# A cross-attention and FFN kernel: scores and skip product in fp16 halves, x fully normalised, keys scaled per batch

## The chip, the cores and the metric

The kernel runs on one core of a Trainium2 chip, as one launch over 32 batches. The metric is the device time of that launch in microseconds (us), median of several runs; lower is better.

## The reference, cut to what matters

```python
def _L0_xattn_ref(pcd_up, pcd_down, Wq, Wk, Wv, Wskip):     # (32,128,1024), (32,128,256)
    q = einsum('oc,bcn->bon', Wq, pcd_up)
    k = einsum('oc,bcm->bom', Wk, pcd_down)
    v = einsum('oc,bcm->bom', Wv, pcd_down)
    energy = einsum('bcn,bcm->bnm', q, k) / sqrt(128)
    attention = softmax(energy, axis=-1)
    x = einsum('bnm,bcm->bcn', attention, v)
    return einsum('oc,bcn->bon', Wskip, pcd_up) + x

x = x + _L0_xattn_ref(_layernorm(x), ctx_1024, Wq, Wk, Wv, Wskip)
x = x + _L0_ffn_ref(_layernorm(x), qweight, scales, zeros, bias)   # 4 bit weights, 1024 -> 1024
```

All of it is in float32.

## The kernel before, in words

A batch is a 128 x 1024 tile of x and a 128 x 256 tile of context. Wq and Wk are multiplied once into one matrix (`proj[:, KEY]`), so that the scores of a batch are x times (KEY x ctx): 1024 rows by 256 columns, made in eight tiles of 128 x 256, two tiles to a chunk `j` of 0 to 3. The chunks alternate between two PSUM tiles `ps_e`.

Precision is kept by splitting operands into a high and a low part, and adding three products (hi hi, hi lo, lo hi; `HI_LO`). Before the change x minus its mean (`xc`), the keys `k` and the skip weights `wsk` are split into two float32r parts; the inverse standard deviation `rstd1` of the layer norm is folded into the keys (`keys_hi`, `keys_lo`) and into `sk_scale`, and `xc` is only centred. The values `v`, the probabilities and the second normalised x (`xn`) are already split into fp16 parts.

The five engines work on different batches at once. The order of work is written out by hand for each engine (its `run_in` for the first batches, then `step(t)` for t from 2), and semaphores tie them together. In `step(t)` TensorE does, with b = t, n = t + 1, a = t - 1, q = t - 2: `scores(b, 0)`, `keys_values(n)`, `skip_attend(a, 0)`, `scores(b, 1)`, `scores(b, 2)`, `skip_attend(a, 1)`, `scores(b, 3)`, `ffn(q, 0)`, `ffn(q, 1)`. `scores(b, 2)` and `scores(b, 3)` use the PSUM tiles of chunks 0 and 1 again and wait for `exp_done` of these.

A chunk's way is: TensorE `scores` (L889), VectorE `row_max` (L659), ScalarE `exps` (L480, one activation a tile with the row sum), VectorE `invert` (L664), GpSimd `normalise` (L255), ScalarE `probs_hi` (L489), VectorE `probs_lo` (L668), two transposing DMAs of SyncE, and TensorE `skip_attend` of the next step (L915 skip, L919 attention).

The first layer norm's way is: VectorE `stats1`, `aggregate1` (L604), `variance1` (L610), GpSimd `inverse_std1` (L263), and ScalarE `centre` (L435) and `centred_hi` (L442), GpSimd `centred_lo` (L270, for the first batch VectorE's `first_centred_lo`, L639). `centre` needs only the mean, not `inverse_std1`.

VectorE's `value_scale` (L621 to L629, four instructions on 128 x 1) reads the context's maximum summed over partitions, which a one-column matmul (L898) leaves in `ps_m`, but waits for `kv_done`, the end of `keys_values`. The second layer norm goes VectorE `residual` (L678), `stats2`, `aggregate2`, GpSimd `inverse_std2` (L279, L281), ScalarE `apply_norm2` (L498) and `xn_high` (L507), GpSimd `xn_low` (L302), SyncE's transposes and TensorE `ffn` (L924, L928).

Of the kernel before, what the change touches and what calls it, by code (L numbers as in the profile page):

```python
# [15 lines left out]
def xattn_ffn_program(nc, x, ctx_in, wq, wk, wv, wskip, qweight, scales, zeros, bias, out):  # L16
# [26 lines left out]
    with es:  # L43
# [73 lines left out]
        st1_done, mv1_done, ve1_done, rstd1_done = (sem(n) for n in ("st1", "mv1", "ve1", "rstd1"))  # L117
        xc_done, xchi_done, xclo_done = (sem(n) for n in ("xc", "xchi", "xclo"))
# [920 lines left out]
```

## Time and profile before

| | |
|---|---|
| median of 3 runs | 526.82 us (526.39 to 528.74) |
| the profiled execution's own time | 526.57 us |
| its span, first to last instruction | 524.6 us (1.97 us lie around it) |
| mean granted TensorE clock | 0.99 |
| busy: TensorE / GpSimd / VectorE / ScalarE | 95% / 90% / 82% / 71% |

Times in the rows below are counted from the start of the span. TensorE's matmuls are pipelined: one of 512 columns is shown as 0.38 us long while the next starts 0.216 us after it. So what a matmul costs is read from the distance of starts, not from its duration, and a matmul that follows without a wait on another group may be shown a little early.

### The profile page before, as it was taken

What the parts mean: (1) busy time and instruction counts of PE and PEld (TensorE: products, weight loads), DVE (VectorE), ACT (ScalarE), POOL (GpSimd) and SP (SyncE); (2) the same over time, 40 slices, a digit from 0 to 9 for tenths busy, and PEclk for the clock granted to TensorE, in tenths of its full rate; (3) what the DMA queues carried; (4) which work ended last, traced back from release to release, by engine and by line L of the source; (5) the groups of instructions that cost most, each with busy time, mean ns of one, the idle gap of its engine ahead of it and who ended that gap; (6) DMA issues with size and microseconds to landing.
All of it is one profiled execution on the core that took longest, in us unless ns stands there. A gap on an engine that the chain in (4) does not pass through costs nothing.

```text
span 524.6 us, 9213 instructions
## 1 busy us (share of the span) xinstructions
PE 496.9 (95%) x2668; PEld 302.8 (58%) x2668; DVE 427.5 (82%) x981; ACT 372.7 (71%) x844; POOL 470.8 (90%) x717
## 2 busy tenths in 40 slices
PE   4658999999999999999999999999999999999977
PEld 3535565656665565666656566666556666656533
DVE  5899788889888888988888898888888988887632
ACT  4878877777877777777777777777777787776610
POOL 4899899999999999999999999999999999999752
PEclk9889999999999999999999999999999999999999
DMA  8626877797898789779878877887787679655673
GB/s 300 191 69 137 161 196 185 190 194 179 178 184 194 167 187 193 192 171 185 204 163 186 182 195 174 192 202 160 184 182 201 174 179 209 159 134 138 147 142 102
DMA packets 227059, 92.65 MB, mean 177 GB/s; under 512 B 209472, under 2 KB 214080, under 8 KB 227008
## 3 DMA queue, kind: packets, MB, share of 16 engines
q1 hardware_dynamic: 226288, 91.91, 74.5%
q8 instruction: 21, 0.34, 0.3%
q14 instruction: 30, 0.25, 0.1%
q10 hardware_dynamic: 720, 0.14, 0.1%
HBM read 23.87 MB, written 16.78 MB: 77 GB/s over the span
## 4 chain that ended last, share of the span: by engine, by line
PE 86%; POOL 7%; DVE 2%; DMA 2%; issue 1%; ACT 1%; POOLq 0%; SPq 0%
PE ps_y L924 41%; PE ps_e L889 15%; PE ps_o L919 14%; PE ps_o L915 8%; PE ps_kv L900 3%; PE ps_y L928 3%; PE ps_kv L902 2%; POOL sb_prob L255 2%; POOL sb_xc_lo L270 1%; DMA sb_xnt_lo<-sb_xn_lo 1%; DMA sb_x<-in_x_dram 1%; POOL sb_xn_lo L302 1%; ACT sb_prob L480 1%; DVE sb_st L596 0%; ACT sb_wf L512 0%
## 5 line engine op out<-in xcount | busy, mean ns | idle before, releaser
L924 PE MATMUL ps_y<-sb_wf,sb_xnt_hi 128*128 128x512 f16 x512 | 192.1, 380 | 4.4 <-DMA sb_xnt_lo<-sb_xn_lo 3.4
L924 PE MATMUL ps_y<-sb_wf,sb_xnt_lo 128*128 128x512 f16 x512 | 192.0, 379 | 0.0
L480 ACT ACTIVATE sb_prob<-ps_e,sb_neg_max 128x256 f32<-128x256 f32 x256 | 118.3, 470 | 57.2 <-DVE sb_neg_max L659 57.2
L255 POOL TENSOR_SCALAR sb_prob<-sb_prob,sb_rsum 128x256 f32<-128x256 f32 x256 | 122.7, 492 | 15.2 <-DVE sb_rsum L664 15.0
L668 DVE TENSOR_TENSOR sb_p_lo<-sb_prob,sb_p_hi 128x1024 f16<-128x1024 f32 x64 | 78.3, 1223 | 48.8 <-ACT sb_p_hi L489 48.8
L889 PE MATMUL ps_e<-sb_k_hi,sb_xc_hi 128*128 128x256 f32 x256 | 90.8, 355 | 10.4 <-DVE sb_k_lo L647 5.7
L249 POOL TENSOR_TENSOR sb_o<-sb_prod,sb_x 128x512 f32<-128x512 f32 x63 | 80.6, 1279 | 7.0 <-DVE sb_prod L702 7.0
L924 PEld LDWEIGHTS ps_y<-sb_wf,sb_xnt_hi 128*128 128x128 f16 x512 | 49.9, 98 | 63.8 <-DMA sb_xnt_lo<-sb_xn_lo 4.3
L659 DVE TENSOR_REDUCE sb_neg_max<-ps_e 128x2 f32<-128x512 f32 x128 | 84.8, 681 | 1.6 <-PE ps_e L889 1.2
L924 PEld LDWEIGHTS ps_y<-sb_wf,sb_xnt_lo 128*128 128x128 f16 x512 | 50.0, 98 | 56.7
L489 ACT ACTIVATE sb_p_hi<-sb_prob 128x1024 f16<-128x1024 f32 x64 | 67.4, 1053 | 19.8 <-issue 15.5
L270 POOL TENSOR_TENSOR sb_xc_lo<-sb_xc,sb_xc_hi 128x512 fp32r<-128x512 f32 x62 | 79.9, 1289 | 0.0
L498 ACT ACTIVATE sb_xn<-sb_x,sb_nb,sb_rstd 128x1024 f32<-128x1024 f32 x32 | 43.0, 1344 | 51.7 <-POOL sb_nb L281 51.7
L889 PE MATMUL ps_e<-sb_k_lo,sb_xc_hi 128*128 128x256 f32 x256 | 73.5, 287 | 0.0
L889 PE MATMUL ps_e<-sb_k_hi,sb_xc_lo 128*128 128x256 f32 x256 | 73.3, 286 | 0.0
L302 POOL TENSOR_TENSOR sb_xn_lo<-sb_xn,sb_xn_hi 128x512 f16<-128x512 f32 x63 | 71.9, 1162 | 0.1
L889 PEld LDWEIGHTS ps_e<-sb_k_hi,sb_xc_hi 128*128 128x128 f32 x256 | 49.8, 195 | 22.3 <-DVE sb_k_lo L647 11.4
L702 DVE TENSOR_TENSOR sb_prod<-ps_y,sb_scale_row 128x512 f32<-128x512 f32 x64 | 43.8, 684 | 14.6 <-PE ps_y L928 13.9
L889 PEld LDWEIGHTS ps_e<-sb_k_lo,sb_xc_hi 128*128 128x128 f32 x256 | 50.0, 195 | 2.3
L480 ACT ACTIVATION_READ_ACCUMULATOR sb_prob<-ps_e,sb_neg_max 128x1 f32 x256 | 51.1, 200 | 0.0
L678 DVE SCALAR_TENSOR_TENSOR sb_x<-ps_o,sb_o_scale,sb_x 128x512 f32<-128x512 f32 x64 | 47.2, 738 | 3.8 <-PE ps_o L919 3.8
L919 PE MATMUL ps_o<-sb_pt_hi,sb_v_hi 128*128 128x512 f16 x128 | 49.3, 385 | 0.7 <-DMA sb_pt_lo<-sb_p_lo 0.7
(123 smaller groups left out, 926.1 us busy)
## 6 DMA issues: line engine op xcount, KB each, us to landing
sb_x<-in_x_dram SPq DMA_DIRECT2D x32, 512.0 KB, 4.0
out_dram<-sb_o SPq DMA_DIRECT2D x64, 256.0 KB, 2.4
sb_ctx<-in_ctx_dram SPq DMA_DIRECT2D x32, 128.0 KB, 2.7
sb_q<-in_L_ffn_qweight_dram SPq DMA_DIRECT2D x4, 512.0 KB, 9.0
sb_pt_hi<-sb_p_hi SPq DMA_TRANSPOSE x64, 3.0
sb_pt_lo<-sb_p_lo SPq DMA_TRANSPOSE x64, 2.8
sb_scale_row<-in_L_ffn_scales_dram SPq DMA_DIRECT2D x1, 512.0 KB, 10.9
sb_xnt_hi<-sb_xn_hi SPq DMA_TRANSPOSE x32, 2.8
```

Source lines behind the costliest of these rows:

```text
L249: pool.tensor_tensor(o_sb[:, c % 2, cols], prod[:, h, :], x1[:, c % 3, cols], ALU.add).then_inc(out_done[h], 1)
L255: last = pool.tensor_scalar(prob[:, j, t, :], prob[:, j, t, :], rsum[:, j, t:t + 1], P_SCALE, ALU.mult, ALU.mult)
L270: last = pool.tensor_tensor(xc_lo[:, n % 3, cols], xc[:, cols], xc_hi[:, n % 3, cols].bitcast(F32), ALU.subtract)
L302: last = pool.tensor_tensor(xn_lo[:, k:k + KT // 2, :], xn[:, k:k + KT // 2, :], xn_hi[:, k:k + KT // 2, :], ALU.subtract)
L480: done = act.activation(prob[:, j, t, :], ps_e[j % 2][:, t, :], ACT.Exp, bias=neg_max[:, j, t:t + 1], accum_out=esum[:, j, t:t + 1])
L489: act.activation(p_hi[:, h, :, :].rearrange("n k (t m) -> n k t m", m=P), prob[:, 2 * h:2 * h + 2, :, :].rearrange("n j t (k m) -> n k (j ...
L659: dve.tensor_reduce(neg_max[:, j, :], ps_e[j % 2][:, :, :], AX.X, ALU.max, negate=True).then_inc(max_done[j], 1)
L668: dve.tensor_tensor(p_lo[:, h, :, :].rearrange("n k (t m) -> n k t m", m=P), prob[:, 2 * h:2 * h + 2, :, :].rearrange("n j t (k m) -> n k ...
L678: dve.scalar_tensor_tensor(x1[:, a % 3, cols], ps_o[h][:, :], o_scale[:, a % 3:a % 3 + 1], x_sb[:, a % 4, cols], ALU.mult, ALU.add).then_i ...
L889: last = pe.matmul(ps_e[j % 2][:, t, :], xc_p[s][:, b % 3, cols], k_p[m][:, b % 2, :], start=i == 0, stop=i == 2)
L919: last = pe.matmul(ps_o[h][:, :], v_p[s][:, a % 3, k * P:(k + 1) * P], pt_p[m][:, h, k, :], start=False, stop=k == MT - 1 and i == 2)
L924: pe.matmul(ps_y[h][:, :], xnt_p[s][:, q % 2, kt, :], wf[:, kt, h * HALF:(h + 1) * HALF], start=kt == 0 and s == 0, stop=False)
```

## The change

x is now normalised fully, times 1024: `centre` has `rstd1` as scale and the product mean x rstd x -1 (`nb1`, from the new `negated_mean1` on VectorE) as bias. Keys and skip weights no longer carry `rstd1`. They get a per-batch scale from a bound on their size, which a second one-column matmul makes; the four instructions of `value_scale` become three of `range_scales`. `xc`, `k` and `wsk` are split into fp16 halves in place of float32r. As the scores come out scaled, `exps` multiplies by `top` (a scale operand of 128 x 1) and first makes the scaled negated maximum `neg_top` by one small activation for each chunk, for which it waits itself. Scaling of the two weights moves to GpSimd. The order of the run-in changes on ScalarE, VectorE and GpSimd.

```diff
-        xc_hi, xc_lo = (sb(n, [P, 3, N], F32R) for n in ("xc_hi", "xc_lo"))
-        k_hi, k_lo = (sb(n, [P, 2, M], F32R) for n in ("k_hi", "k_lo"))
+        xc_hi, xc_lo = (sb(n, [P, 3, N], F16) for n in ("xc_hi", "xc_lo"))
+        k_hi, k_lo = (sb(n, [P, 2, M], F16) for n in ("k_hi", "k_lo"))
-        wsk_hi, wsk_lo = (sb(n, [C, 3, C], F32R) for n in ("wsk_hi", "wsk_lo"))
+        wsk_hi, wsk_lo = (sb(n, [C, 3, C], F16) for n in ("wsk_hi", "wsk_lo"))
...
+            def scale_weights():                                   # GpSimd, was on VectorE
+                pool.wait_ge(w_step, 5)
+                for w in (wv_sb, wskip_sb):
+                    pool.tensor_scalar(w[:, :], w[:, :], rw[:, :], None, ALU.mult).then_inc(w_scaled, 1)
...
                 inverse_std1(0)
+                scale_weights()
                 zero_point_quotient()
...
                 normalise(0, 3)
+                inverse_std1(2)
                 zero_point_remainder()
-                inverse_std1(2)
...
             def centre(n):
-                act.wait_ge(mv1_done, n + 1)
+                act.wait_ge(nb1_done, n + 1)
                 if ran(n, 1):
                     act.wait_ge(xclo_done, n)
-                act.activation(xc[:, :], x_sb[:, n % 4, :], ACT.Identity, bias=mv1[:, 0:1],
-                               scale=-1.0).then_inc(xc_done, 1)
+                act.activation(xc[:, :], x_sb[:, n % 4, :], ACT.Identity, bias=nb1[:, :],
+                               scale=rstd1[:, :]).then_inc(xc_done, 1)
...
             def exps(b, j):
                 act.wait_ge(max_done[j], b + 1)
                 if ran(b, 1):
                     act.wait_ge(plo_done[j // 2], b)
+                top = t_scale[:, b % 3, 1:2]
+                act.activation(neg_top[:, j, :], neg_max[:, j, :], ACT.Copy, scale=top).then_inc(top_done, 1)
+                act.wait_ge(top_done, CHUNKS * b + j + 1)
                 for t in range(TPC):
-                    done = act.activation(prob[:, j, t, :], ps_e[j % 2][:, t, :], ACT.Exp,
-                                          bias=neg_max[:, j, t:t + 1], accum_out=esum[:, j, t:t + 1])
+                    done = act.activation(prob[:, j, t, :], ps_e[j % 2][:, t, :], ACT.Exp, scale=top,
+                                          bias=neg_top[:, j, t:t + 1], accum_out=esum[:, j, t:t + 1])
...
             def run_in():                                          # ScalarE
-                centre(0)
+                first_centre(0)
                 first_centred_hi(0)
                 keys_hi(0)
+                first_centre(1)
                 first_centred_hi(1)
                 keep_projections()
-                centre(1)
                 exps(0, 0)
                 exps(0, 1)
+                centre(1)
                 centred_hi(1)
...
+            def negated_mean1(m):                                  # VectorE
+                dve.wait_ge(rstd1_done, m + 1)
+                if ran(m, 1):
+                    dve.wait_ge(xc_done, m)
+                dve.tensor_scalar(nb1[:, :], mv1[:, 0:1], rstd1[:, :], -1.0, ALU.mult,
+                                  ALU.mult).then_inc(nb1_done, 1)
...
-            def value_scale(n):
-                dve.wait_ge(kv_done, n + 1)
+            def range_scales(n):
+                dve.wait_ge(bound_done, n + 1)
+                if n == 0:
+                    dve.wait_ge(floors_made, 2)
+                    dve.wait_ge(w_step, 5)
+                t = t_scale[:, n % 3, :]
+                dve.tensor_tensor(t, (ps_o[0] if n == 0 else ps_m)[:, HALF - 2:HALF], floors[:, :],
+                                  ALU.max).then_inc(t_step, 1)
+                dve.wait_ge(t_step, 3 * n + 1)
+                dve.reciprocal(t_inv[:, n % 2, :], t).then_inc(t_step, 1)
+                dve.tensor_scalar(o_scale[:, n % 3:n % 3 + 1], t_scale[:, n % 3, 0:1], w_inv[:, :], None,
                                   ALU.mult).then_inc(t_step, 1)
-                dve.wait_ge(t_step, 4 * n + 3)
-                dve.wait_ge(rstd1_done, n + 1)
-                dve.tensor_scalar(sk_scale[:, :], v_scale[:, :], rstd1[:, n % 2:n % 2 + 1], P_SCALE, ALU.mult,
...
+            def key_bound():
+                dve.wait_ge(key_kept, 1)
+                dve.tensor_reduce(kmax[:, :], proj[:, KEY, :], AX.X, ALU.max,
+                                  apply_absolute_value=True).then_inc(kmax_done, 1)
+                dve.wait_ge(kmax_done, 1)
+                dve.tensor_scalar(kmax_row[:, :], kmax[:, 0:1].broadcast_to((P, P)), 1.0 / V_TOP, None,
+                                  ALU.mult).then_inc(kmax_done, 1)
...
                 keep_key()
+                key_bound()
+                negated_mean1(0)
                 context_max(0)
-                scale_weights()
+                weight_norms()
+                range_scales(0)
                 first_centred_lo(0)
...
                 row_max(1, 0)
+                negated_mean1(2)
...
                     invert(b, 1)
+                if ran(m):
+                    negated_mean1(m)
                 if ran(n):
                     keys_lo(n)
...
+            def bound(n, to):                                      # TensorE
+                pe.wait_ge(amax_done, n + 1)
+                peak = amax[:, n % 2:n % 2 + 1]
+                pe.matmul(to[:, HALF - 2:HALF - 1], top_inv[:, :], peak, start=True, stop=True)
+                pe.matmul(to[:, HALF - 1:HALF], kmax_row[:, :], peak, start=True, stop=True).then_inc(bound_done, 1)
```

`keys_hi(n)` now waits for `t_step` (the reciprocal in `range_scales`) where it waited for `rstd1_done`; `weight_norms` is the old reductions without the scaling, with one more reduction. For batch 0 `first_centre` and `first_centred_hi` work on halves of 512 columns. From batch 2 on `keys_values(n)` calls `bound(n, ps_m)` where it had its one-column matmul; for batch 1 `second_keys` does.

## Rows read from the trace of the kernel before

**Rows 1.** The page's first part: busy time, share, instructions.
```profile
PE 496.9 (95%) x2668; PEld 302.8 (58%) x2668; DVE 427.5 (82%) x981; ACT 372.7 (71%) x844; POOL 470.8 (90%) x717
```

**Rows 2.** Windows view, 60 to 490 us: busy by engine, PEclk, DMA.
```profile
60.00:490.00 430.00, 430.00 (x2346) 262.26 (x2346) 365.22 (x842) 319.61 (x738) 405.26 (x592) 1.00 0.79 182
```

**Rows 3.** The chain that ended last, in order of time, three places.
```profile
53.34 1.04 PE ps_y L924 x4
...
203.05 3.47 PE ps_y L924 x16
...
218.26 3.47 PE ps_y L924 x16
```

**Rows 4.** Waits in total, times, longest, window 60 to 490 us.
```profile
ACT sb_prob L480 <- DVE sb_neg_max L659: 55.8, 85, 1.8
...
DVE sb_t_scale L621 <- PE ps_kv L902: 8.1, 26, 0.3
```

**Rows 5.** Timeline of TensorE within one batch: start, duration.
```profile
202.89 0.39 PE L924 MATMUL ps_y<-sb_wf,sb_xnt_hi 128*128 128x512 f16 x1
203.12 0.38 PE L924 MATMUL ps_y<-sb_wf,sb_xnt_lo 128*128 128x512 f16 x1
...
206.57 0.38 PE L924 MATMUL ps_y<-sb_wf,sb_xnt_hi 128*128 128x512 f16 x1
...
209.81 0.38 PE L924 MATMUL ps_y<-sb_wf,sb_xnt_lo 128*128 128x512 f16 x1
...
210.95 0.18 PE L898 MATMUL ps_m<-sb_amax,sb_ones 128*128 128x1 bf16 x1
210.99 0.68 PE L900 MATMUL ps_kv<-sb_ctx,sb_proj 128*128 128x256 f32 x2
...
213.74 0.38 PE L919 MATMUL ps_o<-sb_pt_hi,sb_v_lo 128*128 128x512 f16 x1
...
214.07 0.28 PE L889 MATMUL ps_e<-sb_k_lo,sb_xc_hi 128*128 128x256 f32 x1
...
215.26 0.28 PE L889 MATMUL ps_e<-sb_k_hi,sb_xc_lo 128*128 128x256 f32 x1
215.38 0.40 PE L915 MATMUL ps_o<-sb_xc_hi,sb_wsk_hi 128*128 128x512 f32 x1
...
216.09 0.39 PE L919 MATMUL ps_o<-sb_pt_hi,sb_v_hi 128*128 128x512 f16 x1
```

**Rows 6.** Groups of instructions, 60 to 490 us, ScalarE and GpSimd: busy, mean ns, idle before.
```profile
L480 ACT ACTIVATE sb_prob<-ps_e,sb_neg_max 128x256 f32<-128x256 f32 x230 | 106.3, 471 | 55.8 <-DVE sb_neg_max L659 55.8
L489 ACT ACTIVATE sb_p_hi<-sb_prob 128x1024 f16<-128x1024 f32 x56 | 58.9, 1052 | 13.6 <-issue 13.6
...
L498 ACT ACTIVATE sb_xn<-sb_x,sb_nb,sb_rstd 128x1024 f32<-128x1024 f32 x28 | 37.6, 1344 | 41.6 <-POOL sb_nb L281 41.6
L435 ACT ACTIVATE sb_xc<-sb_x,sb_mv 128x1024 f32<-128x1024 f32 x27 | 30.8, 1141 | 0.0
...
L255 POOL TENSOR_SCALAR sb_prob<-sb_prob,sb_rsum 128x256 f32<-128x256 f32 x226 | 105.9, 481 | 12.1 <-DVE sb_rsum L664 11.9
...
L270 POOL TENSOR_TENSOR sb_xc_lo<-sb_xc,sb_xc_hi 128x512 fp32r<-128x512 f32 x56 | 71.3, 1273 | 0.0
L302 POOL TENSOR_TENSOR sb_xn_lo<-sb_xn,sb_xn_hi 128x512 f16<-128x512 f32 x58 | 66.2, 1162 | 0.0
```

**Rows 7.** Timelines around chunk 1's exponentials and VectorE's `residual`.
```profile
201.41 0.20 ACT L480 ACTIVATION_READ_ACCUMULATOR sb_prob<-ps_e,sb_neg_max 128x1 f32 x1
...
202.30 0.28 PE L889 MATMUL ps_e<-sb_k_lo,sb_xc_hi 128*128 128x256 f32 x1
...
214.42 0.75 DVE L678 SCALAR_TENSOR_TENSOR sb_x<-ps_o,sb_o_scale,sb_x 128x512 f32<-128x512 f32 x1
```

**Rows 8.** Timelines of ScalarE and GpSimd in the run-in.
```profile
14.75 1.06 ACT L442 ACTIVATE sb_xc_hi<-sb_xc 128x1024 fp32r<-128x1024 f32 x1
...
14.26 1.84 POOL L255 TENSOR_SCALAR sb_prob<-sb_prob,sb_rsum 128x256 f32<-128x256 f32 x4 [1.06 <-DVE sb_rsum L664]
```

More of the change, by code:

```diff
@@ L58, in xattn_ffn_program @@
         proj = sb("proj", [C, 3, C])
-        wsum, wmax, rw, w_inv = (sb(n, [C, 1]) for n in ("wsum", "wmax", "rw", "w_inv"))
+        wsum, wskip_max, wmax, rw, w_inv, kmax = (sb(n, [C, 1]) for n in ("wsum", "wskip_max", "wmax", "rw", "w_inv", "kmax"))
         ident, ident16 = sb("ident", [P, P]), sb("ident16", [P, P], BF16)
-        ones = sb("ones", [P, P], BF16)
+        top_inv, kmax_row = sb("top_inv", [P, P], BF16), sb("kmax_row", [P, P], BF16)
+        floors = sb("floors", [P, 2])
         neg_half = sb("neg_half", [P, 1])
@@ L116, in xattn_ffn_program @@
         src_done, rows_turned, rows_done, seed_made = sem("src"), sem("rows_turned"), sem("rows"), sem("seed_made")
[L117 to L118 removed]
+        st1_done, mv1_done, ve1_done, rstd1_done, nb1_done = (sem(n) for n in ("st1", "mv1", "ve1", "rstd1", "nb1"))
+        xc0_done, xc_done, xchi_done, xclo_done = (sem(n) for n in ("xc0", "xc", "xchi", "xclo"))
+        kmax_done, bound_done, top_done = sem("kmax"), sem("bound"), sem("top")
         amax_done, kv_done, t_step, kvhi_done, kvlo_done = (sem(n) for n in ("amax", "kv", "t_step", "kvhi", "kvlo"))
@@ L470, in values_hi @@
                     act.wait_ge(attn_done[1], n - 2)
-                act.activation(wsk_hi[:, n % 3, :], proj[:, SKIP, :], ACT.Copy, scale=sk_scale[:, :])
+                act.activation(wsk_hi[:, n % 3, :], proj[:, SKIP, :], ACT.Copy, scale=t_inv[:, n % 2, 0:1])
                 act.activation(v_hi[:, n % 3, :], ps_kv[:, M:2 * M], ACT.Copy,
-                               scale=v_scale[:, :]).then_inc(kvhi_done, 1)
+                               scale=t_inv[:, n % 2, 0:1]).then_inc(kvhi_done, 1)
             def exps(b, j):
@@ L754, in run_in @@
                 invert(0, 0)
-                value_scale(0)
+                range_scales(1)
+                negated_mean1(1)
                 invert(0, 1)
@@ L786, in run_in @@
                 variance1(3)
-                value_scale(2)
+                range_scales(2)
                 residual(0, 1)
@@ L792, in run_in @@
                 aggregate2(0)
+                negated_mean1(3)
                 keys_lo(2)
@@ L807, in step @@
                 if ran(n):
-                    value_scale(n)
+                    range_scales(n)
                 if t == 2:
@@ L868, in _ @@
             pe.wait_ge(ident_made, 2)
+            pe.wait_ge(kmax_done, 2)
+            bound(0, ps_o[0])
             pe.wait_ge(w_scaled, 2)
@@ L894, in keys_values @@
                 pe.wait_ge(ctx_loaded[n % 2], nth(n, 2))
-                pe.wait_ge(amax_done, n + 1)
                 if ran(n, 1):
                     pe.wait_ge(kvlo_done, n)
-                pe.matmul(ps_m[:, HALF - 1:HALF], ones[:, :], amax[:, n % 2:n % 2 + 1], start=True, stop=True)
                 if n > 1:
+                    bound(n, ps_m)
                     pe.matmul(ps_kv[:, 0:M], proj[:, KEY, :], ctx_sb[:, n % 2, :], start=True, stop=True)
@@ L908, in second_keys @@
                 pe.matmul(ps_y[0][:, 0:M], proj[:, KEY, :], ctx_sb[:, 1, :], start=True, stop=True).then_inc(k1_done, 1)
+                bound(1, ps_m)
             def skip_attend(a, h):
```

91 lines of the change are left out of this document (42 added, 49 removed).

## The prediction

> **What bounds the kernel now.** I read the page's busy shares first [rows 1]: TensorE 95%, GpSimd 90%. Then the windows view of the middle [rows 2]: in those 430 us TensorE is busy all the time at full granted clock, GpSimd 405.26 us (94%), VectorE 85%, ScalarE 74%. Busy matmuls overlap, so this alone doesn't say that TensorE is the bound; the waits do: in this window no wait of TensorE for another engine is listed, while ScalarE waits 55.8 us for row maxima [rows 4] and 41.6 us for the second norm [rows 6]. And the chain that ended last runs through TensorE and repeats exactly: the first half of an `ffn` starts at 203.05 and again at 218.26 [rows 3], so a batch takes 15.21 us, and 430 us hold 28.3 batches. The reader should see two things: time taken out of TensorE's stream comes out of the total, once for each batch; and the others have little room, GpSimd above all.
>
> The first `ffn`, that of step 2, is on the chain from 53.34 [rows 3]. Before it TensorE waits for a run-in in which GpSimd is the bound; after it come the steps 3 to 31, 29 of them with scores.
>
> **What the change takes out of TensorE's stream.** Distances of starts [rows 5]:
> - fp16, 512 columns: 206.57 to 209.81 is 15 steps, 0.216 us each.
> - float32r, 256 columns: 214.07 to 215.26 is 10 steps, 0.119 us each.
> - float32r, 512 columns: 215.38 to 216.09 is 3 steps, 0.237 us each; I take 0.235.
>
> The trace has no fp16 matmul of 256 columns. From below it is half of 0.216, 0.108 us; from above it is what float32r takes, 0.119 (if the weight load or something fixed sets it). The 512 wide ones show a dearer float32r column at equal width (0.235 against 0.216), which a fixed cost for each matmul wouldn't halve at 256 but does (0.019 and 0.011), so I take 0.108. 24 score matmuls a batch x 0.011 = 0.26 us. Six skip matmuls x 0.019 = 0.11 us. Where the stream goes from float32 types to fp16, the first fp16 step is 0.23 (202.89 to 203.12) in place of 0.216; three times a batch, 0.01 each: 0.03 us.
>
> Weighed against this: the Trainium skill (TensorE: Matmul & The Clock Gate, Back-to-back issue gap) says that a warm matmul costs its columns at 2.4 GHz plus 2.5 ns. By it a 256 wide fp16 step is 0.109 us, and the saving of the scores 0.24 in place of 0.26; the trace's 0.216 for 512 columns agrees with it.
>
> Added: the second one-column matmul. The first costs 0.04 us (210.95 to 210.99 [rows 5]). The second has other weights to load behind so short a matmul, so it costs between 0.04 and one small matmul's whole duration, 0.18. I take 0.08. Net: 0.26 + 0.11 + 0.03 - 0.08 = 0.32 us a batch, bounds -0.04 (scores no faster, second column matmul 0.18) and 0.36 (that matmul 0.04). Period 14.89. Over 29 steps: 9.3 us.
>
> **What the others get, and what hides it.**
> GpSimd: 405.26 us in 28.3 batches is 14.33 a batch. `centred_lo` gets the operand types that `xn_low` has, so 1162 in place of 1273 ns [rows 6], twice a batch: 0.22 less. In the steady part `scale_weights` doesn't run and `inverse_std1` is as before. Its idle time without the waits for `invert` [rows 6], (430 - 405.26 - 11.9) / 28.3 = 0.45 a batch, are small gaps between chained one-column instructions and stay. So it needs 14.56, under 14.89. Bound: no saving, 14.78.
>
> VectorE: `sk_scale` goes, `negated_mean1` comes, both about 0.2 us. `range_scales` waits for the one-column matmuls, not for `keys_values`: a wait of 0.3 us (8.1 us in 26 [rows 4]) goes, and with the instruction that goes VectorE reaches `residual(a, 0)` about 0.5 earlier. `negated_mean1(m)` stands behind `invert(b, 1)`, when `inverse_std1(m)` has long been done; `keys_lo` and `values_lo` stand behind it and have slack of microseconds. Free, as VectorE has 15% idle.
>
> ScalarE: the small activation before each chunk. Not in the trace. Below: 0.20, the read of the accumulator [rows 7]; above: 0.47, a 256 column exponential [rows 6]. From 1052 ns at 1024 columns without a 128 x 1 operand and 471 - 89 at 256 (next sentence) a column costs 0.87 ns and the rest 0.16, plus 0.09 for the operand: 0.25. With its own wait I take 0.30. Each exponential has a second 128 x 1 operand: `centre` with one takes 1141 ns, `probs_hi` without 1052 ns, both 1024 columns, so 0.09 each; bounds 0 and 0.20 (the 1344 of `apply_norm2`, with two and a row sum, less 1141). Sum for ScalarE: 4 x 0.30 + 9 x 0.09 = 2.0 us a batch. Its waits are (55.8 + 41.6 + 13.6) / 28.3 = 3.9 us a batch [rows 4, 6], less the 0.32 that the batch shrinks: it fits with 1.6 us to spare. A wait for the maximum is now followed by 0.30 + 2 x 0.09 = 0.48 more before `exp_done`.
>
> The Trainium skill (ScalarE: Activation LUTs, What ACT_TABLE_LOAD costs) speaks against this part of the change in the same way: each pointer operand adds some 93 ns. By it ScalarE's extra comes to about 2.0 us too, and the 89 ns between the rows agrees.
>
> Who waits for `exp_done`? TensorE, before `scores(b, 3)` for chunk 1. Now the last read of the accumulator ends at 201.41 + 0.20 = 201.61, and `scores(b, 3)` starts at 202.30 less one step, 202.18 [rows 7]: slack 0.57 us. Measured from `scores(b, 0)`, the need comes 18 x 0.011 + 0.11 + 0.02 - 0.08 = 0.25 sooner. The maximum can come sooner as well: it stands behind `residual(a, 0)`, which starts at 214.42 though its matmul ended at 213.74 + 0.38 = 214.12 [rows 5, 7]; VectorE's 0.5 lets it start there: 0.3. So slack 0.57 - 0.48 - 0.25 + 0.3 = 0.14 us. No stall, but barely. For chunk 0 there is more: `keys_values`, half of the skip and attention and `scores(b, 1)` lie between.
>
> **The run-in.** Its end is set by GpSimd, which from 14.26 us on [rows 8] has hardly a gap until about 50 us. Changes: `keys_hi(0)` now needs `key_bound` (two instructions of about 0.3), the weight norms (one reduction more) and `range_scales(0)` on VectorE, and `centre` needs `inverse_std1` and `negated_mean1`. Step by step with the durations of the same instructions: the first scores come about 0.85 later; the second half of `first_centred_lo`, and with it `stats1(1)` and the first row maximum, about 1.5 later; the first exponential 1.4 later, and GpSimd's first `normalise` at 15.5 in place of 14.26. `centre(1)` then stands behind two chunks of exponentials: `centred_hi(1)` starts near 17.7 in place of 14.75, `centred_lo(1, 0)` some 2.7 later. Chunks 2 and 3 stand behind that on ScalarE, and GpSimd waits for them; `centre(2)` stands behind `negated_mean1(2)`, itself behind the maximum of batch 1. I get `normalise(1, 0)` 3.6 to 4 us late. GpSimd gets back six times 0.11 by 50 us. I take +3.5 us; bounds +0.8 (only the first scores' delay) and +5.
>
> **Sum.** 526.57 (this execution; the median is 0.25 more) - 9.3 + 3.5 = 520.8. This is the likeliest, with 516.5 to 524.5 as its own range (0.25 to 0.37 a batch, gain 7.3 to 10.7; run-in 0.8 to 5).
>
> **Rivals.**
> A. *The exponentials' chain becomes the bound* (slower). Place: `scores(b, 3)` waits for `exp_done` of chunk 1. For: slack of 0.14 only. Against: ScalarE and VectorE each have slack elsewhere. At the upper bounds (small activation 0.47 and 0.05 for its wait, operands 0.20 each) 0.92 is added in place of 0.48, which is 0.30 more than the slack of 0.14 takes: a stall of 0.30 a batch, 8.8 us, 529.6. It makes the kernel slower than before from a stall of 0.20, 0.82 added. Chance 0.14.
> B. *GpSimd becomes the bound.* If `centred_lo` is no faster (14.78) and its waits for `invert`, 11.9 us or 0.42 a batch [rows 6], stay in part, its period is 14.95 to 15.20: gain 7.5 to 0.3, time 522.6 to 529.8, middle 526. For: 94% busy. Against: the same types run at 1162 ns. Chance 0.12.
> C. *A 256 column matmul is no cheaper in fp16*, so that the change doesn't do in the scores what it says: 0.06 a batch, 1.8 us, time 528.3. Chance 0.06.
> D. *The run-in hardly costs*: the first maxima come late, but ScalarE has its first exponentials earlier in its order than `centre(1)`, and if GpSimd's small zero-point steps fill its waits, only +0.8 stays: 518. Chance 0.14.
> Chance of the likeliest 0.54.
>
> **How the numbers follow.** A measurement of this kernel tells a change of about 0.5%, 2.6 us. Faster by more than that means under 524.2: the likeliest (0.50 of 0.54), D (0.14), the near end of B (0.04): 0.68. Within: the rest of the likeliest (0.04), most of B (0.06), most of C (0.04), the small stalls of A (0.02): 0.16. Slower than 529.2: A with its stall near the bound (0.12), and the far ends of B and C (0.04): 0.16. Range for 8 in 10: from 515, as the run-in and the steps could both come out at their best, to 528, which leaves out A at its bound and the far ends.
>
> **What the profile after would show.** Right: starts of score matmuls 0.108 to 0.109 apart, skip 0.216; period 14.85 to 14.9; no wait of TensorE in the window 60 to 490; `centred_lo` near 1160 ns; exponentials near 560 ns and four small activations near 0.28; the first `ffn` 3 to 4 us later than 53.34. Wrong: a regular gap of TensorE ahead of `scores(b, 3)` released by ScalarE (A), period over 14.95 with GpSimd without a gap (B), 0.119 steps (C), a first `ffn` by 54.5 (D).

## The result, and the profile after

The changed kernel takes 546.33 us, median of 4 runs (546.22 to 546.45), beside 527.57 us (526.39 to 528.74) for the kernel before: ratio 1.036, 95% interval 1.033 to 1.038. It is slower by 19 us, where 520.8 was predicted. The profiled execution took 546.41 us, its span is 544.5. Two executions of run 13 below (587 and 588 us, granted clock 0.84 in place of 0.98) and one of run 11 (2917 us) were in a slower state, and are not counted.

First part of the page after, then the windows view of 60 to 490 us, against [rows 1, 2]:

```profile
PE 491.4 (90%) x2668; PEld 265.9 (49%) x2700; DVE 420.8 (77%) x982; ACT 433.8 (80%) x973; POOL 481.0 (88%) x721
...
ACT 34%; DVE 20%; issue 17%; POOL 15%; PE 2%; DMA 1%; SPq 0%; ACTq 0%; another core or an unknown queue 0%; POOLq 0%
```

```profile
60.00:490.00 430.00, 413.06 (x2276) 224.55 (x2302) 348.78 (x819) 361.77 (x817) 402.08 (x576) 1.00 0.83 176
```

TensorE now has gaps, and makes up 2% of the chain that ended last, which [rows 3] showed running through its `ffn`. No engine is busy all the time: ScalarE has the largest share of the chain, 34%, and is busy 361.77 of 430 us. So I looked for a loop over several engines: each waits for the one before it, and none is busy throughout.

The period is read from the distance of one instruction of each batch, GpSimd's bias of the second norm (`inverse_std2`, L281 before, L289 after). Its timeline after:

```profile
106.29 1.26 POOL L289 TENSOR_SCALAR sb_nb<-sb_mv,sb_rstd 128x1 f32<-128x1 f32 x1
...
483.34 1.26 POOL L289 TENSOR_SCALAR sb_nb<-sb_mv,sb_rstd 128x1 f32<-128x1 f32 x1
```

24 batches lie between: 15.71 us each, where the kernel before has 15.22 (99.51 to 479.91 us, 25 batches). And the view of this tile, with shortest, median and longest duration in ns and the first and last start, has the first at 42.4 us where before it was at 38.1 (second line):

```profile
L289 POOL TENSOR_SCALAR sb_nb<-sb_mv,sb_rstd x32: 267/1258/1264, 42.4 to 527.1; 128x1 f32<-128x1 f32 x32
```

```profile
L281 POOL TENSOR_SCALAR sb_nb<-sb_mv,sb_rstd x32: 265/748/752, 38.1 to 506.2; 128x1 f32<-128x1 f32 x32
```

So the run-in costs 4.3 us and the 31 periods behind it 16.6 (484.7 less 468.1); the tail gives 1 back. (The prediction named another sign of the run-in, the part of the first `ffn` that starts at 53.34 [rows 3]: it starts at 57.79 after, 4.5 later.)

The groups that answer to [rows 6], 60 to 490 us, and the waits of the same window:

```profile
L492 ACT ACTIVATE sb_prob<-ps_e,sb_neg_top,sb_t_scale 128x256 f32<-128x256 f32 x217 | 120.6, 560 | 3.6
...
L278 POOL TENSOR_TENSOR sb_xc_lo<-sb_xc,sb_xc_hi 128x512 f16<-128x512 f32 x54 | 62.5, 1157 | 0.0
...
L289 POOL TENSOR_SCALAR sb_nb<-sb_mv,sb_rstd 128x1 f32<-128x1 f32 x27 | 34.0, 1259 | 2.7
L489 ACT ACTIVATE sb_neg_top<-sb_neg_max,sb_t_scale 128x2 f32<-128x2 f32 x109 | 32.1, 294 | 23.1 <-DVE sb_neg_max L687 23.0
```

```profile
PEld ps_e L932 <- ACT sb_prob L492: 30.1, 47, 1.4
DVE sb_rsum L692 <- ACT sb_prob L492: 28.9, 54, 0.6
ACT sb_neg_top L489 <- DVE sb_neg_max L687: 23.0, 54, 0.6
PE ps_e L932 <- ACT sb_prob L492: 13.5, 24, 0.9
```

The single costs came out near what was worked out: an exponential 560 ns (predicted 471 + 89), the small activation 294 (predicted 0.28 to 0.30), `centred_lo` 1157 (1162). TensorE's wait for the exponentials is there, as rival A had it. The row to look at is the second wait: VectorE's `invert` waits for the exponentials 54 times in 27 batches, twice in each. And `nb` of the second norm takes 1259 ns where it took 748, though nothing in it changed.

Timelines of VectorE, ScalarE and GpSimd after, around the last chunk of a batch. In brackets stands the idle time before an instruction and what ended it:

```profile
197.39 0.17 DVE L692 RECIPROCAL sb_rsum<-sb_esum 128x2 f32<-128x2 f32 x1
197.47 0.73 DVE L706 SCALAR_TENSOR_TENSOR sb_x<-ps_o,sb_o_scale,sb_x 128x512 f32<-128x512 f32 x1
198.12 0.68 DVE L687 TENSOR_REDUCE sb_neg_max<-ps_e 128x2 f32<-128x512 f32 x1
...
200.40 0.17 DVE L692 RECIPROCAL sb_rsum<-sb_esum 128x2 f32<-128x2 f32 x1 [0.56 <-ACT sb_prob L492]
200.48 1.21 DVE L696 TENSOR_TENSOR sb_p_lo<-sb_prob,sb_p_hi 128x1024 f16<-128x1024 f32 x1
```

```profile
198.83 0.30 ACT L489 ACTIVATE sb_neg_top<-sb_neg_max,sb_t_scale 128x2 f32<-128x2 f32 x1 [0.43 <-DVE sb_neg_max L687]
...
200.17 0.20 ACT L492 ACTIVATION_READ_ACCUMULATOR sb_prob<-ps_e,sb_neg_top,sb_t_scale 128x1 f32 x1
201.85 1.36 ACT L510 ACTIVATE sb_xn<-sb_x,sb_nb,sb_rstd 128x1024 f32<-128x1024 f32 x1 [1.49 <-POOL sb_nb L289]
```

```profile
199.91 0.55 POOL L287 TENSOR_TENSOR sb_rstd<-sb_ve,sb_neg_half 128x1 f32<-128x1 f32 x1 [0.21 <-DVE sb_ve L721]
200.56 1.26 POOL L289 TENSOR_SCALAR sb_nb<-sb_mv,sb_rstd 128x1 f32<-128x1 f32 x1
```

The same place before, VectorE, ScalarE and GpSimd:

```profile
203.57 0.67 DVE L659 TENSOR_REDUCE sb_neg_max<-ps_e 128x2 f32<-128x512 f32 x1
...
205.12 0.15 DVE L693 TENSOR_SCALAR sb_ve<-sb_mv 128x1 f32<-128x1 f32 x1
205.33 0.17 DVE L664 RECIPROCAL sb_rsum<-sb_esum 128x2 f32<-128x2 f32 x1
205.41 1.21 DVE L668 TENSOR_TENSOR sb_p_lo<-sb_prob,sb_p_hi 128x1024 f16<-128x1024 f32 x1
```

```profile
205.09 0.20 ACT L480 ACTIVATION_READ_ACCUMULATOR sb_prob<-ps_e,sb_neg_max 128x1 f32 x1
```

```profile
206.00 0.75 POOL L281 TENSOR_SCALAR sb_nb<-sb_mv,sb_rstd 128x1 f32<-128x1 f32 x1
```

From the start of `row_max(b, 3)` to that of `invert(b, 3)` it is 1.76 us before and 2.28 after: 0.52 more, the small activation with its hand-over (0.33) and two operands (0.18). Before, VectorE came to this `invert` just as the exponentials ended (205.27 and 205.29), with no idle time and no slack either. After, it idles 0.56 us there, and all that stands behind it in its order moves: `probs_lo(b, 0)`, `context_max`, `scale_product(q, 0)`. GpSimd's `nb`, which starts beside `probs_lo`, ends 0.13 us after it (201.82 and 201.69), as before (206.75 and 206.62). So it too follows the exponentials, and `apply_norm2`, which ScalarE has in its order ahead of the next batch's work, starts at 201.85.

The whole loop stands in the chain of waits of after, in order of time (start, us), here with its middle:

```profile
301.00 0.30 ACT sb_neg_top L489
...
303.55 0.95 ACT sb_xc_hi L457
304.50 0.19 ACT sb_neg_top L489
...
305.18 0.75 ACT sb_prob L492 x3
...
307.37 0.17 DVE sb_rsum L692
307.53 0.65 DVE sb_x L706
...
309.89 0.56 POOL sb_rstd L287
...
310.54 1.27 POOL sb_nb L289
...
311.83 0.91 ACT sb_xn L510
...
313.27 0.96 ACT sb_p_hi L501
...
315.39 0.68 DVE sb_prod L730
```

Chunk 0's exponentials, ScalarE's high parts, chunks 1 and 2, `invert`, `residual(a, 1)`, the second norm, `apply_norm2`, `probs_hi`, `probs_lo`, `scale_product`, and the row maximum of the next chunk 0. TensorE is not in it. Chunk 3's exponentials are not in it either, as this view follows semaphores: by the rows above they come in through `probs_lo`, with whose end `nb` ends.

### The profile page after: what moved, and what is told of

It reads as the page before. It is cut to its first block, busy times and chain, and to the rows that moved or that the text cites. A ratio compares the mean times of both kernels' runs of the same rounds, so it can differ in the third digit from the quotient of the medians.

```text
span 544.5 us, 9380 instructions
## 1 busy us (share of the span) xinstructions
PE 491.4 (90%) x2668; PEld 265.9 (49%) x2700; DVE 420.8 (77%) x982; ACT 433.8 (80%) x973; POOL 481.0 (88%) x721
## 4 chain that ended last, share of the span: by engine, by line
ACT 34%; DVE 20%; issue 17%; POOL 15%; PE 2%; DMA 1%; SPq 0%; ACTq 0%; another core or an unknown queue 0%; POOLq 0%
ACT sb_prob L492 11%; POOL sb_nb L289 7%; ACT sb_xn L510 6%; ACT sb_p_hi L501 5%; ACT sb_xc_hi L457 5%; DVE sb_neg_max L687 4%; DVE sb_x L706 4%; DVE sb_st L711 4%; DVE sb_prod L730 4%; POOL sb_prob L259 4%; POOL sb_rstd L287 3%; ACT sb_neg_top L489 3%; PE ps_y L967 2%; DVE sb_rsum L692 2%; ACT sb_k_hi L472 2%
## 5 line engine op out<-in xcount | busy, mean ns | idle before, releaser
L492 ACT ACTIVATE sb_prob<-ps_e,sb_neg_top,sb_t_scale 128x256 f32<-128x256 f32 x256 | 142.3, 560 | 4.2
L259 POOL TENSOR_SCALAR sb_prob<-sb_prob,sb_rsum 128x256 f32<-128x256 f32 x256 | 124.9, 501 | 21.2 <-DVE sb_rsum L692 18.2
L932 PE MATMUL ps_e<-sb_k_hi,sb_xc_hi 128*128 128x256 f16 x256 | 71.8, 280 | 29.5 <-ACT sb_prob L492 17.8
L278 POOL TENSOR_TENSOR sb_xc_lo<-sb_xc,sb_xc_hi 128x512 f16<-128x512 f32 x62 | 72.7, 1173 | 1.2 <-ACT sb_xc_hi L457 1.1
L932 PE MATMUL ps_e<-sb_k_lo,sb_xc_hi 128*128 128x256 f16 x256 | 71.3, 278 | 0.0
L932 PE MATMUL ps_e<-sb_k_hi,sb_xc_lo 128*128 128x256 f16 x256 | 71.3, 278 | 0.0
L489 ACT ACTIVATE sb_neg_top<-sb_neg_max,sb_t_scale 128x2 f32<-128x2 f32 x128 | 37.6, 294 | 29.8 <-DVE sb_neg_max L687 29.7
L692 DVE RECIPROCAL sb_rsum<-sb_esum 128x2 f32<-128x2 f32 x128 | 19.7, 154 | 45.2 <-ACT sb_prob L492 42.9
L932 PEld LDWEIGHTS ps_e<-sb_k_hi,sb_xc_hi 128*128 128x128 f16 x256 | 25.4, 99 | 58.7 <-ACT sb_prob L492 36.0
## 6 DMA issues: line engine op xcount, KB each, us to landing
sb_scale_row<-in_L_ffn_scales_dram SPq DMA_DIRECT2D x1, 512.0 KB, 10.5
```

Source lines behind the costliest of these rows:

```text
L259: last = pool.tensor_scalar(prob[:, j, t, :], prob[:, j, t, :], rsum[:, j, t:t + 1], P_SCALE, ALU.mult, ALU.mult)
L492: done = act.activation(prob[:, j, t, :], ps_e[j % 2][:, t, :], ACT.Exp, scale=top, bias=neg_top[:, j, t:t + 1], accum_out=esum[:, j, t:t ...
L932: last = pe.matmul(ps_e[j % 2][:, t, :], xc_p[s][:, b % 3, cols], k_p[m][:, b % 2, :], start=i == 0, stop=i == 2)
```

## The experiments

Two theories. **L**: the loop over VectorE, ScalarE and GpSimd has taken TensorE's place; what counts is where a step stands. **S**: the rival; what counts is ScalarE's work in sum, wherever it stands. The first four runs ask before that whether it is the exponentials at all.

**1. The exponentials as before.** `exps` of after without the small activation and without the scale operand. Here and in runs 2, 3, 5 and 6 the softmax is left unscaled, so the output differs. That this doesn't set the time is seen from runs 4 and 8, which show the same two things with the right softmax.

```diff
-                top = t_scale[:, b % 3, 1:2]
-                act.activation(neg_top[:, j, :], neg_max[:, j, :], ACT.Copy, scale=top).then_inc(top_done, 1)
-                act.wait_ge(top_done, CHUNKS * b + j + 1)
...
-                    done = act.activation(prob[:, j, t, :], ps_e[j % 2][:, t, :], ACT.Exp, scale=top,
-                                          bias=neg_top[:, j, t:t + 1], accum_out=esum[:, j, t:t + 1])
+                    done = act.activation(prob[:, j, t, :], ps_e[j % 2][:, t, :], ACT.Exp,
+                                          bias=neg_max[:, j, t:t + 1], accum_out=esum[:, j, t:t + 1])
```

> The changed kernel with the exponentials of the kernel before: no small activation, no scale operand (the scores stay unscaled inside the softmax, so its output differs). Theory L: a loop over VectorE and ScalarE (row maximum, exponentials of chunks 1 and 3, then the reciprocal that stands in VectorE's order ahead of the values' low half and of the probabilities' low half, the second norm, ScalarE's second norm application, the next batch) sets the period of 15.71 us; each of chunks 1 and 3 gives back 0.33 + 2 x 0.09 = 0.51, so the loop needs 14.69 and TensorE's own 14.87 is the bound: about 519 to 522 us. Rival G: GpSimd or the transposes set the period (nb2 takes 1.26 us, transposes land in 4.2 us): over 538 us. Rival R: the run-in alone has the loss: it stays over 540.

517.58 us, ratio to the kernel before 0.983 (0.979 to 0.987); period 14.88. The whole loss and more, 28.8 us, is in these lines (L had 519 to 522). Its windows view and the chain in shares:

```profile
60.00:490.00 430.00, 428.10 (x2398) 241.66 (x2426) 365.14 (x853) 329.26 (x750) 406.54 (x607) 1.00 0.86 185
```

```profile
PE 81%; POOL 5%; DVE 4%; ACT 3%; issue 3%; DMA 2%; SPq 1%; another core or an unknown queue 0%; POOLq 0%; ACTq 0%; DVEq 0%
```

TensorE is the bound again, and what the prediction says of its stream holds: 14.88 against 14.89 predicted.

**2 and 3. One of the two at a time.** Run 2 keeps the scale operand alone (a column of ones), run 3 the small activation alone, with its wait.

```diff
+                    ... ACT.Exp, scale=one_col[:, :], bias=neg_max[:, j, t:t + 1], ...          # run 2
...
+                act.activation(neg_top[:, j, :], neg_max[:, j, :], ACT.Copy, scale=one_col[:, :]).then_inc(top_done, 1)
+                act.wait_ge(top_done, CHUNKS * b + j + 1)                                         # run 3
```

> The changed kernel without the small activation and its wait, but with a scale operand of 128 x 1 (a column of ones; output differs). Theory L: the loop gets back 2 x 0.33, period 15.05, 31 periods: 526 us. Rival W (only the wait on itself stalls ScalarE, the operand is free): 521. Rival G: over 538.

> The changed kernel with the small activation and its wait, and the exponentials with an immediate scale (the small one multiplies by a column of ones; output differs). Theory L: the loop gets back 4 x 0.09, period 15.35: 535 us. Rival W: 546, nothing is got back. Rival G: over 538.

Run 2: 524.0 us, 0.994 (0.992 to 0.996), period 15.01, 2 us under what was expected. Run 3: 529.0, 1.004 (1.002 to 1.006), period 15.16, 6 us under it. Over run 1 the two cost 6.4 and 11.4 us, 17.8 in sum, and 28.8 together. So each alone seems first to use up slack that the two must share; runs 5 and 6 say how much.

**4. The same on the kernel before.** Both steps added there, with a scale of one: float32r, keys and `value_scale` as they were.

> The kernel before, with the small activation (times a column of ones) and the scale operand (ones) added, same results. Theory L: its loop is at most 0.3 us under its period of 15.21 (VectorE's wait for the end of keys and values), so 1.02 added gives 15.9 to 16.2: 545 to 556 us. The prediction's view (0.57 us of slack at TensorE, ScalarE with 3.9 us idle): 527 to 530. Rival G or R: 527.

550.8 us, 1.045 (1.041 to 1.049), period 15.88. This is the prediction's own step, tried alone. It held the step to be covered, which would give 527 to 530; it costs 24 us.

**5 and 6. Which chunks.** Both steps (with ones) on chunks 1 and 3 alone, and on chunks 0 and 2 alone; the others as in run 1. Each has half of ScalarE's extra work.

```diff
+                if j in (1, 3):          # run 6: (0, 2)
+                    act.activation(neg_top[:, j, :], neg_max[:, j, :], ACT.Copy, scale=one_col[:, :]).then_inc(top_done, 1)
...
+                else:                    # the exponentials as before
```

> The changed kernel with small activation and scale operand (times a column of ones) on chunks 1 and 3 alone; chunks 0 and 2 have the exponentials of the kernel before (output differs). Theory L (only the chunks whose reciprocal VectorE waits for ahead of the values' low half and of the probabilities' low half count): period near 15.6 to 15.7, 543 to 546 us. Rival S (ScalarE's whole work of a batch counts, all chunks alike): halfway between 517.6 and 546.3, 532 us.

> The same on chunks 0 and 2 alone (output differs). Theory L: period 14.9 to 15.0, 518 to 521 us. Rival S: 532 us.

On 1 and 3: 535.49 us, 1.015 (1.013 to 1.018), period 15.47. On 0 and 2: 520.37, 0.986 (0.984 to 0.989), period 14.87, TensorE's own. The same work costs 2.8 us over run 1 at one place and 17.9 at the other, so S falls. L's numbers hold for 0 and 2, but chunks 1 and 3 were to cost nearly all (543 to 546), and cost 17.9 of 28.8. The timeline of run 5 tells why the other two chunks count once these are there (ScalarE, then VectorE):

```profile
313.72 0.29 ACT L493 ACTIVATE sb_neg_top<-sb_neg_max,sb_one_col 128x2 f32<-128x2 f32 x1 [0.29 <-DVE sb_neg_max L695]
```

```profile
300.73 0.48 DVE L690 SCALAR_TENSOR_TENSOR sb_v_lo<-ps_kv,sb_t_inv,sb_v_hi 128x256 f16<-128x256 f32 x1
301.13 0.15 DVE L700 RECIPROCAL sb_rsum<-sb_esum 128x2 f32<-128x2 f32 x1
```

Chunk 1's step waits 0.29 us for VectorE: chunk 0's 0.52 more on ScalarE would cost 0.23 here. And `invert(b, 2)` doesn't wait for chunk 2, it follows `values_lo` without idle time: part of chunk 2's 0.52 is covered there too. Chunks 1 and 3 show no such cover. If they have none, the loop without any extra is 15.47 - 2 x 0.52 = 14.43 us, by run 5. This is an estimate: no run shows the loop at that length, as TensorE sets the period then. The others by it: run 1, 14.43, under TensorE's 14.88, so TensorE sets it (measured 14.88); run 6, with the 0.24 that after has over run 5, 14.7, under it as well (14.87); run 3, with 0.33 in place of 0.52, 14.43 + 0.66 and a few hundredths for chunks 0 and 2, 15.1 to 15.2 (15.16); run 2, with 0.18, 14.8, so TensorE's 14.88 (15.01, more than both). Most of what is missing there stands in VectorE's `wsk_lo`, which lies ahead of `invert(b, 2)` in its order: in the mean it takes 517 ns in run 2, 420 in run 3, 345 in run 5 and 344 after, though it is the same instruction in all of them. With its 0.17, run 2 comes to 14.96. With all four it is 15.71, 0.24 over run 5, where 0.23 for chunk 0 and something more for chunk 2 was to be expected. By the same reckoning the kernel before had a loop of some 15.88 - 1.04 - 0.24 = 14.6 us (run 4), 0.6 under its 15.22: single waits without slack don't yet make a loop without slack.

**7, 9 and 10. Other orders of VectorE's steps.** If `invert` holds up what stands behind it, another order should bring the loss back. All three are the changed kernel otherwise. Run 7: `negated_mean1`, `keys_lo` and `values_lo` ahead of `invert(b, 1)`, and `probs_lo(b, 0)` ahead of `invert(b, 3)`. Run 9: `context_max` and `scale_product(q, 0)` between `invert(b, 3)` and `probs_lo(b, 0)`. Run 10: run 9, and `invert(b, 1)` behind `values_lo`, `invert(b, 2)` behind `residual(a, 1)` and `row_max(b, 3)`.

> The changed kernel, all of it, but in VectorE's step the reciprocal of chunk 1 comes after keys_lo and values_lo, and that of chunk 3 after probs_lo(b, 0); keys_lo waits for kvhi_done so that the two engines don't read one bank at once. Same results. Theory L: both in-order waits (0.50 and 0.56 us a batch) leave the loop, period 14.9 to 15.1, 521 to 527 us. Rival S: 546, the work on ScalarE is the same. Rival G (normalise comes later, GpSimd takes over): 530 to 540.

542.83 us, 1.029 (1.027 to 1.032), period 15.61: only 3.5 us of it. L's 521 to 527 is far off, and the time alone lies between G's 530 to 540 and S's 546, of which runs 5 and 6 exclude S. `probs_lo` now lies on the other small step of GpSimd (VectorE, then GpSimd):

```profile
214.00 1.22 DVE L696 TENSOR_TENSOR sb_p_lo<-sb_prob,sb_p_hi 128x1024 f16<-128x1024 f32 x1
```

```profile
214.16 1.46 POOL L287 TENSOR_TENSOR sb_rstd<-sb_ve,sb_neg_half 128x1 f32<-128x1 f32 x1
...
215.72 0.27 POOL L289 TENSOR_SCALAR sb_nb<-sb_mv,sb_rstd 128x1 f32<-128x1 f32 x1
```

The power, 0.55 us elsewhere, takes 1.46, and `nb` 0.27. So what was saved in one was lost in the other, as far as these rows go.

> The changed kernel, all of it, but in VectorE's step context_max and scale_product(q, 0) come between the reciprocal of chunk 3 and probs_lo(b, 0). Same results. Theory L2 (the loop runs through chunks 0, 1 and 2 on ScalarE, residual, second norm; and its last link, GpSimd's nb2 of 0.27 us, is stretched to 1.26 because it starts while VectorE's probs_lo runs and ends with it): nb2 is back to about 0.27, the loop loses 1.0, period 14.9 to 15.1, 521 to 527 us. Rival H (nb2 is not held by probs_lo but slow for another reason, or ScalarE's work sets the period): nb2 stays over 0.7 and the time over 540.

535.84 us, 1.015 (1.012 to 1.018), period 15.35. With `probs_lo` out of the way of both steps the second norm comes about 1 us sooner, and 10.5 us come back: this link was real, and H is out. But the time is 9 us over L2's range, not at TensorE's bound. GpSimd's groups in the window:

```profile
L253 POOL TENSOR_TENSOR sb_o<-sb_prod,sb_x 128x512 f32<-128x512 f32 x56 | 97.8, 1747 | 2.3 <-DVE sb_prod L730 2.2
...
L299 POOL CAST sb_xn_lo<-sb_rs 128x3 bf16<-128x3 f32 x28 | 33.0, 1180 | 0.0
L289 POOL TENSOR_SCALAR sb_nb<-sb_mv,sb_rstd 128x1 f32<-128x1 f32 x28 | 7.4, 264 | 2.8
```

`nb` is down from 1259 to 264 ns, but `write_out`'s product now lies beside `probs_lo` and went from 1272 to 1747 twice a batch, and a three-column cast takes 1180, which took 0.20 (L299 at 203.91 us after). GpSimd is busy 410.9 of 430 us and has 41% of the chain that ended last (15% after), so it is most of the next bound; VectorE's `invert` still waits 31.6 us for exponentials.

> The same, and the reciprocals of chunks 1 and 2 stand behind values_lo and behind residual(a, 1) and row_max(b, 3), so that no exponential lies ahead of the second norm in VectorE's order (keys_lo waits for kvhi_done). Same results. Theory L2: TensorE's bound, period 14.87 to 14.95, 520 to 523 us. Rival G (normalise of chunks 1 and 2 comes later and GpSimd sets the period): 15.1 or more, over 526.

550.0 us, 1.043 (1.040 to 1.046), period 15.86: in rival G's range, not L2's. GpSimd's `normalise` needs these `invert`s, and now waits for them 30.9 us in the window (11.4 after), while GpSimd is busy 391.69 of 430 us only. So not its own work sets the period but its waits, which this order adds: something waits for these `invert`s on each side.

**8, 11, 12 and 13. The halves without scaled exponentials.** Run 8 has the fp16 halves, but x times 4 in place of 1024 and the keys times 1/4, with no per-batch bound: the scores come out in their own size and `exps` is that of before. The second one-column matmul, `key_bound` and the key scale go.

```diff
+    X1_SCALE = 4.0
-                dve.tensor_scalar(ve1[:, :], mv1[:, 1:2], EPS, XN_SCALE ** -2 ...
+                dve.tensor_scalar(ve1[:, :], mv1[:, 1:2], EPS, X1_SCALE ** -2 ...
...
-                dve.tensor_scalar(proj[:, KEY, :], ps_o[0][:, 0:C], SM_SCALE / XN_SCALE, None,
+                dve.tensor_scalar(proj[:, KEY, :], ps_o[0][:, 0:C], SM_SCALE / X1_SCALE, None,
```

> fp16 halves without scaled exponentials: x normalised times 4, keys divided by 4 and unscaled, so the scores come out right and the exponentials are those of the kernel before; one column matmul only, no key bound. Theory L: TensorE's bound, period 14.85, 14.4 of it saved run-in work or less: 515 to 518 us. Rival: the fp16 parts cost elsewhere: over 520.

520.4 us (517.74 to 521.01), 0.985 (0.981 to 0.989), period 14.87: faster than both kernels, with the period that L had. The time is 2.4 us over its range of 515 to 518, which had hoped for run-in work saved: the first `nb` is at 40.8 us, still 2.7 later than before.

Run 11 gives it the order of run 9. Run 12 has besides, in the run-in, the weights scaled on VectorE again and `range_scales(0)` later; run 13 has this run-in without the other order.

> Unscaled exponentials with fp16 halves (x times 4, keys divided by 4) and the order of the gap run. Theory L2: already at TensorE's bound without the order, so within 1.5 us of 520.4: 519 to 521.

> The same, and in the run-in the two weights are scaled on VectorE again (not on GpSimd, where it took 0.62 and 0.99 us) and range_scales(0) stands behind the first halves. The first scores come about 1 us sooner and GpSimd's zero-point steps start sooner: 1 to 2 us less than the run beside it, 518 to 519. Rival: the run-in's end is set elsewhere, no difference.

> The halves with the exponentials as before (x times 4), in the steps' order of the changed kernel, and in the run-in the two weights scaled on VectorE again with range_scales(0) behind first_centred_lo(1) and scale_inverse. GpSimd's two scalings take 1.6 us of the run-in, VectorE's 0.6. If GpSimd's stretch up to 50 us sets when the steady part begins, this comes 1 to 1.5 us earlier than the same kernel without the edit (520.4): 518.5 to 519.5. If the late centre(1) on ScalarE sets it, there is no difference: 520 to 521.

Run 11: 527.3 us, 0.999 (0.996 to 1.001), period 15.07, where 519 to 521 was expected. The order that gave the changed kernel 10 us takes 7 from this one, as GpSimd pays for it (`write_out` 1701 ns in place of 1271; GpSimd has 69% of the chain). Run 12: 527.5, 1.000 (0.999 to 1.002), no difference from run 11, as its rival said. Run 13: 519.9 and 520.6 in two executions, 0.988 (0.983 to 0.992), just over the range expected; the first `nb` is 0.7 us earlier than in run 8 (40.1 against 40.8), its span 1.2 shorter, and in the time that is within run 8's spread. So what this change of the run-in is worth, about 1 us, isn't settled.

**14. The small step on VectorE.** The changed kernel, with `neg_top` made on VectorE right behind each row maximum.

```diff
             def row_max(b, j):                                     # VectorE
...
+                dve.wait_ge(top_done, CHUNKS * b + j + 1)
+                dve.tensor_scalar(neg_top[:, j, :], neg_max[:, j, :], t_scale[:, b % 3, 1:2], None,
+                                  ALU.mult).then_inc(max_done[j], 1)
```

> The changed kernel with the scaled negated maximum made on VectorE right behind each row maximum, not by ScalarE; the exponentials keep both operands, results unchanged. Theory L (a loop of single steps over VectorE, ScalarE and GpSimd sets the period, so a step counts on whichever of the three engines it stands): the small step is about as long on VectorE and stands there four times a batch, so hardly anything comes back: 538 to 547, period 15.45 to 15.75. Rival S (it is the work standing on ScalarE, in its order, that counts; VectorE has 23% idle): the 4 x 0.3 us come back and the time is that of the scale operand alone, 524, or a little over: 523 to 530, period 15.0 to 15.2.

576.0 us, 1.093 (1.089 to 1.097), period 16.76 (94.20 to 479.65 us, 23 batches): slower by 30 us than with the step on ScalarE. S falls for good, ScalarE is busy 315.48 of 430 us here. L was right that nothing comes back, but its 538 to 547 is far too low. VectorE and GpSimd:

```profile
301.09 0.23 DVE L688 TENSOR_SCALAR sb_neg_top<-sb_neg_max,sb_t_scale 128x2 f32<-128x2 f32 x1
...
305.48 0.72 DVE L688 TENSOR_SCALAR sb_neg_top<-sb_neg_max,sb_t_scale 128x2 f32<-128x2 f32 x1
...
309.37 0.89 DVE L688 TENSOR_SCALAR sb_neg_top<-sb_neg_max,sb_t_scale 128x2 f32<-128x2 f32 x1
```

```profile
309.08 1.16 POOL L278 TENSOR_TENSOR sb_xc_lo<-sb_xc,sb_xc_hi 128x512 f16<-128x512 f32 x1
```

Alone the step takes 0.23 us; beside GpSimd's `centred_lo` it ends with that (310.26 and 310.24). Mean 509 ns, four times a batch, in the order of the engine that has most links of the loop (54% of the chain). That is 0.7 us a batch more than the step took on ScalarE (4 x 0.33), of the 1.05 that the period grew; the rest isn't placed.

**All in all.** Of the 14 runs only 4 and 6 came out in the range that L or L2 had stated. So the loop's length is not known well enough to forecast by. What the runs do show is the sign and the place: the two steps of `exps` cost the time (1, 4, 8), chunks 1 and 3 cost 15 us more than 0 and 2 for the same work (5, 6), `nb` behind `probs_lo` is a link (9), and ScalarE's work in sum isn't the measure (5, 6, 14). That the loop runs through `invert` and what stands behind it in VectorE's order is read from the rows and the chain, and agrees with runs 5, 6 and 9; no order of these steps that was tried frees the loop.

## Why the prediction was wrong

**TensorE's stream: right.** Score steps are 0.110 us apart after (predicted 0.108), skip steps 0.216, and the second one-column matmul costs 0.03 where I took 0.08. Runs 1, 6 and 8 have periods of 14.87 to 14.88, predicted 14.89.

**The run-in: near in number, 0.8 short.** +4.3 us against +3.5, within the bounds of 0.8 to 5. Rival D is out. In run 1, without the two steps in `exps`, the first `nb` is at 40.5, 2.3 later than before: so some 2 us of the 4.3 come with these two steps, more than the working gave them.

**The single costs on ScalarE: right** (0.33 with its wait for 0.30; 0.09 for each operand), and so 0.51 for a chunk in place of 0.48.

**"Who waits for `exp_done`? TensorE": this is the step that failed.** I followed the added 0.48 us to one waiter only. VectorE's `invert(b, 1)`, `invert(b, 2)` and `invert(b, 3)` wait for the same semaphores; in the trace of before the first and the last ran with neither idle time nor slack (the exponentials of chunk 1 end at 201.61 [rows 7], `invert(b, 1)` starts at 201.67), the second with 0.3 us (ends at 202.51, starts at 202.85), and behind them in VectorE's order stand `residual(a, 1)`, `probs_lo` and `scale_product`:

```profile
201.67 0.15 DVE L664 RECIPROCAL sb_rsum<-sb_esum 128x2 f32<-128x2 f32 x1
...
202.85 0.14 DVE L664 RECIPROCAL sb_rsum<-sb_esum 128x2 f32<-128x2 f32 x1
```

They don't show in [rows 4], as a waiter that comes just in time has no waiting time. Runs 5, 6 and 4 show the cost at this place: 15.1 us between chunks 1 and 3 and chunks 0 and 2 for equal work, 24 us on the kernel before.

**"It fits with 1.6 us to spare": right as a sum, and no argument.** ScalarE was busy 84% of the window after and still had the largest share of the chain. Its idle time, the 55.8 and 41.6 us in [rows 4, 6], was not room: it was the other parts of a loop. The right question was how long the way from one `apply_norm2` to the next is, through all engines: an estimated 14.43 us in the changed kernel without the extras, from run 5, so 0.45 under TensorE's new period of 14.88, against 2 x 0.52 added at uncovered places and 0.24 for the other two chunks.

**Rival A** had the right cause and direction, and TensorE does wait as it said. But it put the place at `scores(b, 3)`. That isn't where the time is lost: after the wait the last matmul of `scores(b, 3)` ends at 212.53 (one batch after the rows above), and VectorE comes to `row_max(b, 3)` at 213.83 only.

```profile
212.26 0.27 PE L932 MATMUL ps_e<-sb_k_hi,sb_xc_lo 128*128 128x256 f16 x1
```

It put the price at 0.30 a batch at the upper bounds of the costs; the costs came out in the middle, and the period is 0.83 over TensorE's 14.88. So even rival A had the direction by a path that doesn't bind. B didn't occur here (GpSimd idles more than before), but it is close behind, as runs 9 and 11 show. C is out.

## What to carry to other kernels

For each step that gets longer, list every instruction in every engine's order that waits for its semaphore, those above all that wait for it without idle time, and what stands behind them. Then measure the way round from one batch's instruction to the next batch's same one through all engines: idle time of an engine that is spent waiting for others in such a loop is not room. A scale that makes numbers fit a format is best folded where it costs no instruction on that way, as a constant; here x times 4, whose scores come out in their own size, was 26 us cheaper than x times 1024 with scaled exponentials. It gives up the per-batch scale of the keys, and no run here tells how it does on inputs of another size.

## What the runs showed of the hardware

In all these rows a GpSimd instruction that starts during VectorE's `probs_lo` (two inputs in SBUF, 1.21 us) ends after it, however small: `nb` of 128 x 1 took 0.26 us alone, 0.75 before and 1.26 after, the power 0.55 and 1.46, a cast of 128 x 3 0.20 and 1.18. The reverse holds too: VectorE's step of 128 x 2 took 0.23 alone and 0.89 when it started in `centred_lo`. So the cost is not that of the instruction but what is left of the other's: from the start of `row_max(b, 3)`, `nb` starts 2.43 us later before and 2.44 after, and ends 3.18 and 3.70 later, as `probs_lo` starts 0.52 later.

The Trainium skill (SBUF — State Buffer, Who interferes with whom) says that a VectorE instruction with two SBUF inputs contends with a GpSimd one that reads SBUF, that a `tensor_scalar` in a two-port mode does so as well, and that whichever comes second blocks until the first has ended. The ends of the rows above agree, 0.13 us apart for `nb` and 0.02 for VectorE's step, though the power in run 7 ends 0.40 behind `probs_lo`. No row tells which mode VectorE's step ran in.

A second one-column matmul with other weights, right behind a first, put the next matmul off by 0.02 to 0.03 us, though each is shown 0.16 to 0.17 long.
